# Seven of sixteen expert pairs scattered to a side table, ten shared down products behind the pairs, and half of the table sums on GpSimd

## What is computed

```python
slot = jnp.where(pos < C, flat_e * C + pos, E * C)
xb = zeros.at[slot].set(x[tok_idx]).reshape(E, C, h)
g, u = jnp.split(jnp.einsum('ech,ehf->ecf', xb, w_gate_up), 2, axis=-1)
yb = jnp.einsum('eci,eih->ech', silu(g) * u, w_down)
out = jnp.einsum('tk,tkh->th', topk_w, yb[slot])       # 6 rows per token
gs, us = jnp.split(x @ ws_gate_up, 2, axis=-1)
out = out + (silu(gs) * us) @ ws_down                  # shared expert
...
x = layernorm(x + out)
```

## Time and profile before

| | |
|---|---|
| median of 3 runs | 1086.15 us (1084.98 to 1086.78) |
| the profiled execution's own time | 1092.47 us |
| its span, first to last instruction | 1090.7 us |
| busy: PE, DVE, ACT, POOL | 93%, 78%, 64%, 59% of the span |
| mean granted clock of PE | 0.973 of full |
| DMA engines | 75.42 MB, mean 69 GB/s |

### The profile page before, as it was taken

The page is one execution under the profiler, slowest core; times in us unless marked ns, Lnnn a source line. Parts: engine busy times, 40 slices in busy tenths (PEclk is TensorE's granted clock), DMA queues, the critical chain, the costliest instruction groups (busy, mean ns, idle before and its releaser), DMA issues.

```text
span 1090.7 us, 17557 instructions
## 1 busy us (share of the span) xinstructions
PE 1019.1 (93%) x6072; PEld 809.2 (74%) x6072; DVE 850.7 (78%) x1391; ACT 698.9 (64%) x1162; POOL 647.2 (59%) x660
## 2 busy tenths in 40 slices
PE   7799999999999999999999999999999968899966
PEld 5588878887888788888878887888788747345532
DVE  6579898989898889888988898889988865833423
ACT  4667777777777777777777777777777752323212
POOL 2536666666666666666666666666666662365332
PEclk9999999999999999999999999999999987999987
DMA  5610011101110101010101000100000007739937
GB/s 193 238 30 20 31 39 30 62 30 39 31 61 30 41 30 61 31 40 30 62 30 40 31 20 30 40 30 20 21 20 21 21 1 227 209 86 265 237 55 235
DMA packets 52168, 75.42 MB, mean 69 GB/s; under 512 B 8208, under 2 KB 43248, under 8 KB 51952
## 3 DMA queue, kind: packets, MB, share of 16 engines
q1 hardware_dynamic: 48144, 69.30, 20.1%
q0 software_dynamic: 3072, 4.46, 2.2%
q10 hardware_dynamic: 864, 0.54, 0.2%
HBM read 63.00 MB, written 15.75 MB: 72 GB/s over the span
## 4 chain that ended last, share of the span: by engine, by line
PE 67%; DVE 16%; issue 6%; DMA 6%; POOL 2%; ACT 2%; SPq 0%; ACTq 0%; DVEq 0%; POOLq 0%
PE ps L462 19%; PE ps L463 18%; PE ps L464 18%; DVE prob_lo L1230 6%; PE ps L499 5%; DMA acc_rows<-ye,acci 4%; PE ps L676 2%; DVE qraw L1299 2%; POOL pacc L1089 2%; PE ps L720 2%; PE ps L767 1%; DVE qraw L1317 1%; DVE kT_lo L1230 1%; PE ps L716 1%; DVE qhat_lo L1230 1%
## 5 line engine op out<-in xcount | busy, mean ns | idle before, releaser
L1230 DVE TENSOR_TENSOR prob_lo<-praw,prob_hi 128x1024 fp32r<-128x1024 f32 (+7 forms) x256 | 301.4, 1201 | 3.4 <-ACT prob_hi L837 3.4
L1072 POOL TENSOR_SCALAR_AFFINE_SELECT praw<-praw 128x128 f32<-128x128 f32 x256 | 119.5, 467 | 264.4 <-ACT praw L893 261.6
L1089 POOL TENSOR_TENSOR pacc<-pacc,praw 128x768 f32<-128x768 f32 (+2 forms) x192 | 234.6, 1222 | 27.7
L887 ACT ACTIVATE praw<-ps,rk 128x1024 f32<-128x1024 f32 (+7 forms) x256 | 186.2, 741 | 68.8 <-PE ps L464 64.6
L837 ACT ACTIVATE prob_hi<-praw 128x1024 fp32r<-128x1024 f32 (+7 forms) x256 | 168.7, 686 | 1.9 <-POOL praw L1072 1.9
L893 ACT ACTIVATE praw<-praw 128x1024 f32<-128x1024 f32 (+7 forms) x256 | 168.2, 684 | 0.0
L462 PE MATMUL ps<-qhat_hi,kT_hi 128*128 128x512 f32 (+3 forms) x384 | 135.2, 352 | 9.6 <-DVE qhat_lo L1230 9.6
L462 PE MATMUL ps<-prob_hi,vS_hi 128*128 128x512 f32 (+3 forms) x384 | 136.4, 355 | 8.0 <-DVE prob_lo L1230 8.0
L463 PE MATMUL ps<-prob_lo,vS_hi 128*128 128x512 f32 (+3 forms) x384 | 133.9, 349 | 0.0
L464 PE MATMUL ps<-prob_hi,vS_lo 128*128 128x512 f32 (+3 forms) x384 | 133.0, 346 | 0.0
L463 PE MATMUL ps<-qhat_lo,kT_hi 128*128 128x512 f32 (+3 forms) x384 | 132.9, 346 | 0.0
(11 more groups left out here) (167 smaller groups left out, 2240.2 us busy)
## 6 DMA issues: line engine op xcount, KB each, us to landing
qsq<-rq_rows SPq DMA_DIRECT2D x32, 512.0 KB, 4.0
wgu<-in_wgu SPq DMA_DIRECT2D x16, 704.0 KB
wd<-in_wd SPq DMA_DIRECT2D x16, 352.0 KB
acc_rows<-acc_rows SPq DMA_DIRECT2D x8, 544.0 KB, 6.1
acc_rows<-pacc SPq DMA_DIRECT2D x8, 512.0 KB, 9.8
accA<-acc_rows SPq DMA_DIRECT2D x8, 512.0 KB, 5.8
wraw<-in_wqkv SPq DMA_DIRECT2D x15, 256.0 KB, 4.5
wvraw<-in_wqkv SPq DMA_DIRECT2D x16, 128.0 KB, 2.7
```

What stands on the lines that cost most here:

```text
L887: nc.scalar.activation(praw[:, raw_at(b, j)], buf[:, P * j:T], ACT.Tanh, scale=rk[:, b, j:j + 1]).then_inc(tanh_done, 1)
L1072: nc.gpsimd.affine_select(out=diag, in_=diag, compare_op=ALU.is_ge, fill=0.0, base=0, pattern=[[1, P]], channel_multiplier=-1).then_inc(ma ...
L1089: nc.gpsimd.tensor_tensor(pacc[:, P * j:T], before, raw, ALU.add).then_inc(pacc_done, 1)
L1230: v.tensor_tensor(dst, x_, hi.bitcast(F32), ALU.subtract).then_inc(done, 1)
```

## The change

It reorders the stage after the attention and rebalances its work:

- All 12 shared units run ahead of the loop: one more ahead of the merge product, unit 11 after the slot product.
- In the pair loop gate/up runs two pairs ahead and the turn one pair ahead of the down product. Shared down 0 stands ahead of gate/up 0, five more in pairs 2 to 6. The other ten run after the loop into sum banks, each of which a product of zeros (`open_bank`, bf16, `zrow`) clears first.
- The side table takes pairs 1, 3, ... 13, the main table the other nine. `ye` has 8 entries. The side loads are ordered so that one quarter of `yacc` after the other is complete, and DVE adds them all after the loop.
- `accB` is no tensor of its own but lies over the weights of three ring entries; so SP waits for `egu_done` of all pairs ahead of the table loads, no longer for the shared downs.
- For odd k POOL adds accA and accB (`tables_added`) and PE adds only the sum.

```diff
-SHARED_SECOND = 7
-SHARED_THIRD = 8
-SHARED_FOURTH = 11
-FILL_UP = {1: 11}
-FILL_DOWN = {0: 0} | {p: p - 1 for p in range(2, 13)}
-ADDED = len(FILL_DOWN)
-SLOT_TURNS = {1: 1, 4: 2, 7: 3}
-SIDE = [p for p in range(WR) if p % 2]
+SHARED_SECOND = 8
+SHARED_THIRD = 9
+YE = 8
+FILL_FIRST = 0
+FILL_DOWN = {p: p - 1 for p in range(2, 7)}
+ADDED = 1 + len(FILL_DOWN)
+SLOT_TURNS = {1: 1, 5: 2, 9: 3}
+SIDE = [p for p in range(14) if p % 2]
 MAIN = [p for p in range(PAIRS) if p not in SIDE]
-SIDE_ADDS = {11: (0, 1), 12: (2, 3), 14: (4, 5), 15: (6, 7)}
-SUM_BANKS = [0, 1, 4, 5, 6, 7, 2, 3]
+SUM_BANKS = [2, 3, 1, 4, 5, 0, 6, 7]
...
-        ye = sb("ye", [P, 4, D])
+        ye = sb("ye", [P, YE, D])
+        zrow = sb("zrow", [32, P + 512], BF16)
...
-        accB = sb("accB", [P, NT, D])
+        accB = wgu[:, 0:3].rearrange("p w u c f -> p (w u c f)")[:, 0:NT * D].rearrange("p (i d) -> p i d", d=D)
...
-                four = slice(4 * (n % 4), 4 * (n % 4) + 4)
-                sp.dma_start(accA[:, four, :], side_v[n // 4][:, four, :]).then_inc(side_in[n], 16)
+                into, four = slice(4 * (n % 4), 4 * (n % 4) + 4), slice(4 * (n // 2), 4 * (n // 2) + 4)
+                sp.dma_start(accA[:, into, :], side_v[n % 2][:, four, :]).then_inc(side_in[n], 16)
             sp.wait_ge(side_done, 8)
             sp.wait_ge(added, 16 * len(MAIN))
-            sp.wait_ge(sd_done, NT)
+            sp.wait_ge(egu_done, PAIRS)
...
+            def open_bank(k):
+                mm(ps[:, SUM_BANKS[k], :], zrow[:, 0:P], zrow[:, P:P + 512], start=True, stop=False)
...
             for n in range(KC):
                 slots_turned(n)
+            shared_down(FILL_FIRST)
             gate_up(0)
+            gate_up(1)
+            turn_act(0)
             for p in range(PAIRS):
+                if p + 2 < PAIRS:
+                    gate_up(p + 2)
                 if p + 1 < PAIRS:
-                    gate_up(p + 1)
-                turn_act(p)
-                if p in FILL_UP:
-                    shared_up(FILL_UP[p])
+                    turn_act(p + 1)
                 if p in FILL_DOWN:
                     shared_down(FILL_DOWN[p])
-                expert_down(p)
                 if p in SLOT_TURNS:
                     for c in range(KC):
                         slots_turned(SLOT_TURNS[p] * KC + c)
+                expert_down(p)
...
             for k in range(ADDED // 2, NT // 2):
+                open_bank(k)
+                shared_down(2 * k)
+                shared_down(2 * k + 1)
...
             for k in range(NT // 2):
-                pe.wait_ge(acc_in[k], 32)
-                add_rows(k, accA, False, False)
-                add_rows(k, accB, False, True).then_inc(sum_done, 1)
+                if k % 2:
+                    pe.wait_ge(acc_added, k // 2 + 1)
+                else:
+                    pe.wait_ge(acc_in[k], 32)
+                    add_rows(k, accB, False, False)
+                add_rows(k, accA, False, True).then_inc(sum_done, 1)
...
+            def tables_added(k):
+                two = slice(2 * k, 2 * k + 2)
+                pool.wait_ge(acc_in[k], 32)
+                nc.gpsimd.tensor_tensor(accA[:, two, :], accA[:, two, :], accB[:, two, :], ALU.add).then_inc(acc_added, 1)
+
+            tables_added(1)
             for k in range(NT // 2):
+                if k % 2 and k + 2 < NT // 2:
+                    tables_added(k + 2)
                 pool.wait_ge(var2, k + 1)
```

More of the change, by code:

```diff
@@ L742, in _ @@
             last.then_inc(slot_done, 1)
-            for n in range(SHARED_THIRD, SHARED_FOURTH):
+            for n in range(SHARED_THIRD, SHARED_UNITS):
                 shared_up(n)
@@ L751, in slots_turned @@
                     pe.wait_ge(xg_in[q], 16 * 4)
[L752 to L753 removed]
+                if n >= 2:
+                    pe.wait_ge(xbt_read, n - 1)
                 for r in range(4):
[L755 removed]
+                    last = nc.tensor.transpose(ps[:, 1 + 2 * (n % 2), P * r:P * r + P], xg[:, 4 * q + r, P * c:P * c + P], ident[:, :])
                 last.then_inc(xbt_done, 1)
@@ L1004, in _ @@
             nc.scalar.activation(wts[:, :, :], wts[:, :, :], ACT.Exp).then_inc(e_done, 1)
-            for n in range(2, SHARED_FOURTH):
+            for n in range(2, SHARED_UNITS):
                 shared_halves(n)
@@ L1169, in _ @@
             pool.wait_ge(pads, PADS)
+            nc.gpsimd.memset(zrow[:, :], 0.0).then_inc(zrow_set, 1)
             def shared_product(n):
@@ L1188, in scatter @@
                         pool.wait_ge(side_zeros, 16 * 8)
-                    nc.gpsimd.indirect_dma_start(acc2_d, row, ye[:, p % 4, :], None, compute_op=ALU.add).then_inc(side_added, 16)
+                    nc.gpsimd.indirect_dma_start(acc2_d, row, ye[:, p % YE, :], None, compute_op=ALU.add).then_inc(side_added, 16)
                 else:
@@ L1192, in scatter @@
                         pool.wait_ge(added, 16 * MAIN.index(p))
-                    nc.gpsimd.indirect_dma_start(acc_d, row, ye[:, p % 4, :], None, compute_op=ALU.add).then_inc(added, 16)
+                    nc.gpsimd.indirect_dma_start(acc_d, row, ye[:, p % YE, :], None, compute_op=ALU.add).then_inc(added, 16)
             for n in range(SHARED_THIRD):
@@ L1201, in _ @@
                 gather(p)
-            for n in range(SHARED_THIRD, SHARED_FOURTH - 1):
+            for n in range(SHARED_THIRD, SHARED_UNITS - 1):
                 shared_product(n)
@@ L1621, in turned, with add_side @@
                 v.tensor_copy(actT[:, p % 2].rearrange("f k s -> f (k s)"), ps[0:FH, 0, 0:2 * P]).then_inc(et_read, 1)
-            def add_side(n, shared):
+            def add_side(n):
                 dve.wait_ge(side_in[n], 16)
-                dve.wait_ge(sd_added, shared)
-                if n >= 4:
-                    dve.wait_ge(side_done, n - 3)
-                four = slice(4 * (n % 4), 4 * (n % 4) + 4)
-                v.tensor_tensor(yacc[:, four, :], yacc[:, four, :], accA[:, four, :], ALU.add).then_inc(side_done, 1)
+                if n:
+                    dve.wait_ge(side_done, n)
+                into, four = slice(4 * (n % 4), 4 * (n % 4) + 4), slice(4 * (n // 2), 4 * (n // 2) + 4)
+                v.tensor_tensor(yacc[:, four, :], yacc[:, four, :], accA[:, into, :], ALU.add).then_inc(side_done, 1)
             def add_shared(i):
                 dve.wait_ge(sd_done, i + 1)
-                v.tensor_tensor(yacc[:, i, :], yacc[:, i, :], ps[:, 2 + i % 2, 0:D], ALU.add).then_inc(sd_added, 1)
+                v.tensor_tensor(yacc[:, i, :], yacc[:, i, :], ps[:, 2, 0:D], ALU.add).then_inc(sd_added, 1)
             for n in range(KC):
@@ L1639, in _ @@
             dve.wait_ge(x1_out, 16 * B)
+            add_shared(FILL_FIRST)
             product(0)
@@ L1646, in _ @@
                     add_shared(FILL_DOWN[p])
-                for n in SIDE_ADDS.get(p, ()):
-                    add_side(n, min(p, ADDED))
                 if p in SLOT_TURNS:
@@ L1651, in _ @@
                         slots_turned(SLOT_TURNS[p] * KC + c)
+            dve.wait_ge(sd_added, ADDED)
+            for n in range(8):
+                add_side(n)
             for k in range(NT // 2 + 1):
```

60 lines of the change are left out of this document (24 added, 36 removed).

## The result

| | before | changed kernel |
|---|---|---|
| median of the runs of one comparison, us | 1086.47 (4 runs) | 1074.33 (4 runs, 1070.70 to 1075.22) |
| ratio, 95% interval | | 0.9873 [0.9836, 0.9909] |
| the profiled execution's own time | 1092.47 | 1075.17 |
| its span | 1090.7 | 1073.4 |
| selection product to the end of the span | 146.9 | 132.3 |

1.3% faster, by 13.8 us [9.9, 17.8] on 1086.47; the forecast was 17. Measured again in another comparison, the changed kernel came to 0.9884 [0.9861, 0.9908]. The span's end, 1073.4, is the forecast to 0.1 us, and that is partly luck.

The account below looks back on a forecast made before the run. The prediction took the serial main-table scatter-adds, then the tail, to bound the kernel's end. Table loads 15.2 us sooner (1 us loop loss included) plus 2.0 in the tail made 17.2 off: 1069 us, 80% range 1062 to 1078.

Parts of the forecast that it names:

- Balance: Scatters in the pair loop: seven side, nine main; last side landing at 1034, last main near 1045.
- Loop start: Start of the pair loop: near 971.5 instead of 970.5, 1 us lost, bounds 0 and 3 us lost.
- Ten late downs: Behind the pair loop: ten shared downs (13 us) run until 1042 beside the scatters and cost nothing.
- Side loads and adds: After the last side landing at 1034: last add ends at 15.5, plus 0.3; all is added at 1049.8.
- Table loads: After the side adds: SP starts the table loads at 1049.8 instead of 1065.0, 15.2 us gained.
- Tail: First table load to span end: loads end last, 23.7 us instead of 25.7, 2.0 gained (bounds 3 gained, 6 lost).
- The held scatter: Rival: pair 15's scatter is held until all eight side adds are through; gain 15.5, 1070.6 us; chance 0.11.
- the rule weighed: GpSimd and a DVE operation with two SBUF inputs take the same ports in turns, each for a whole instruction.
- The median: Whole kernel: the same 17 us taken off the median of the runs, 1086.15, giving 1069 us.
- own range: Whole kernel: the forecast's range of times, 1066 to 1073 us, given chance 0.53.
- The rival "slower": Side chain: seven links over 10.7 us each put the table loads past 1067; at 11.5 us, 1092 us; chance 0.03.

Follow-up runs that it names:

- the twelve-link chain: Changed kernel with the side table for pairs 1, 3, 5, 7 only, so 12 main scatters again: ratio 0.9988, stage 146.6 us.
- adds on TensorE: Changed kernel with TensorE adding both pieces of every k and no adds on GpSimd: ratio 0.9911, stage 133.9 us.
- before, seven side pairs: Kernel before, with the side table for pairs 1, 3 ... 13 and all eight side adds behind pair 15: ratio 1.0047, stage 147.3 us.
- four side pairs: Changed kernel with the side table for pairs 1, 3, 5, 7 only, all else kept: ratio 0.9988, stage 146.6 us.
- the tables' own place: Changed kernel with the main table's first half loaded into three more weight-ring entries instead of accA: ratio 0.9868, repeated 0.9833.
- without the late weights: Changed kernel without the weight loads of pairs 8 to 15, which reuse earlier weights and compute something else: ratio 0.9847, stage 126.4 us.

## Why the prediction was right, and what was off

*Balance.* Right: the side chain of seven ends 91.4 and 90.2 us into the stage (forecast 90.2), and the twelve-link chain brings the old time back. By itself the balance gave nothing (1.0047), which a sum with no price for the order of the late downs can't tell. A landing under load came to some 8 us (1009.35 to 1017.52), 7.5 assumed; at the end 3.8.

*Loop start.* 2.3 us lost for 1, in the bounds; with a start 1.7 us earlier the side loads did not come sooner. The loss beyond 1 us is the clock, 0.57 granted behind the wait (12.26 us for 10.57); it fell only in profiles where TensorE had also stood idle some 20 us earlier, and no run varies that idle time by itself.

*Ten late downs.* The step "hide beside the scatters, cost nothing" named the cover but not the purpose. What counts is not that ten are late (four late ones did as well in the stage) but that the late ones and the table loads no longer wait behind the side adds. That wait is 9.5 us in the other order.

*Side loads and adds.* 16.3 and 16.0 us for 15.8.

*Table loads.* 107.7 and 106.2 for 106.0: 13.5 and 15.0 us gained, 15.2 forecast.

*Tail.* This step failed. "The loads end last, no longer TensorE" gave 23.7 us; 24.6 and 24.2 were measured, against 25.7 before. The bound is DVE, with `lnv` held by GpSimd's add, in the ring of `lnv`, GpSimd's power and GpSimd's add. Of the 2.0 us forecast 1.1 and 1.5 came. Without GpSimd's adds the last product comes 19.0 us (adds on TensorE) and 18.8 us (before, seven side pairs) after the first table load, both at a granted clock of 1.00, for the 19.9 of before. So the clock alone can give 0.9 to 1.1 us of it: "before, seven side pairs" has the tail of before, and what differs is that TensorE worked ahead of it. What GpSimd's adds bring on top stays open. With four side pairs the tail begins at a granted 0.57, as before, and takes 18.2 us for 19.9. Four profiles with this tail lie at 18.2 to 18.8, but two at 20.1 and 20.4, where the clock fell to about 0.6 after TensorE had waited 2.5 and 2.8 us for the first add.

*The held scatter.* It was not held. Pair 15's scatter was issued at 1037.28 and took 1.55 us, while DVE ran four side adds from 1037.33 on, 1.32 us each with the gaps; neither is longer than alone, although the rule weighed has each keep the ports for a whole instruction. Where the scatter began after the adds had begun it took 0.3 to 0.9 us more (1.84 to 2.46), not the 2.7 of the earlier trace rows. The row of 4.25 us wasn't seen again, and what made it stays open. The changed kernel's side adds, and a scatter that was held, in the repeated run with the tables' own place (five adds there from 1036.10 on):

```profile
1037.33 5.28 DVE L1640 TENSOR_TENSOR yacc<-yacc,accA 128x1024 f32<-128x1024 f32 x4 [12.68 <-DMA accA<-acc_rows]
```

```profile
1036.46 2.29 POOL L1198 DMA_INDIRECT acc_rows<-ye,acci  x1 [4.72 <-DMA acc_rows<-ye,acci]
```

GpSimd and DVE did get in each other's way some 20 us later, on an instruction of DVE that I had not costed.

*The median.* 1069 forecast, 1074.33 measured, so the time is outside the own range of 1066 to 1073 and inside the 80% one. The step that failed is the transfer: 17 us from one execution that ran 6.3 us over its median were taken off the median unchanged. Of the difference of the two spans, 17.3, 2.7 lie in the untouched attention, and the stage itself gave 14.6 and 16.5. The medians give 13.8 and, in the other comparison, 12.6 us. As the kernel before was profiled once, no run shows how much of its 6.3 us lies in the stage.

*A sum that doesn't close.* The rival "slower" puts the last landing past 1052 with seven links of more than 10.7 us. Counted from its own first side issue, 985, seven such links end at 1059, and 9.7 would do. The changed kernel's links stayed at 9.0 or less (983.76 to 992.73, 1000.42 to 1009.35), so nothing hangs on it.

No version that computes all of the reference was shown to be faster than the changed kernel by more than the intervals. The nearest is the one with the tables' own place, with 2 to 6 us less in the stage and a ratio of 0.9868 and 0.9833. Not tried: taking `lnv` off DVE, or putting it where no add runs. The two full holds after 1062, 0.98 less 0.17 us each, make that an estimated 1.6 us at most, since TensorE or the loads may take the bound over.

## What to carry to other kernels

Moving work from a long serial chain to a short one paid here only when what else waited at the end was moved ahead of the new end; the rest of the change alone measured 0.9988, the balance alone 1.0047, together 0.9873. So before balancing chains, list what stands behind each wait in the queues of the engines that will newly wait. When an engine that is not the bound takes over half of another's work, price the smallest instructions of the third engine in the ring too: a 0.17 us one, held to the end of a 1.3 us add in two of the last six pieces, ate much of the help.

## What the hardware showed that I had not expected

- A DVE `tensor_scalar` of 128x2 that began behind a GpSimd add of 128x512 took up to 1.21 us instead of 0.17, by how much of the add was left, and ended 0.01 to 0.04 us after it. This happened at least twice in every profile with such adds, and never in before, before with seven side pairs and adds on TensorE.
- Scatter-adds of 128 rows of 1 KB landed in about 8 us while the late weights moved (1009.35 to the release of 1017.52), and in 3.7 without other traffic (1061.27 before); without the late weights a landing held up none but the last scatter from 998 us on.
- The same three units behind the same 1.40 us wait took 12.26 us in six profiles (12.27 in one of them) and 10.57 in four, of kernels alike up to there. The granted clock behind the wait was 0.54 to 0.57 in the six and 1.00 in the four, and only the six had 1.33 us of idle TensorE some 20 us earlier as well.
- Eight loads of 512 KB issued together were through no sooner than the same loads four at a time: 15.1 to 16.1 us to the start of the last add in three profiles, 15.0 and 15.6 in two.
